# A six-layer local-attention stack on one core: the mask is written into the score banks by ScalarE instead of by two matmuls, and three engines' lists are reordered

## What is computed

```
q, k, v = split(shift_tokens(x) @ Wqkv)        # 16 heads of 64
q, k = l2norm(q) * qs, l2norm(k) * ksc         # then rotary tables, cos and sin part
sim = q @ k2.T * 8                             # windows of 32 queries see 64 keys: the one before and their own
sim = where(mask, -huge, sim)
x = softmax(sim) @ v2 @ Wo + x
x = (a * gelu(gate)) @ W2 + b2 + x             # (a, gate) = layernorm(shift_tokens(x)) @ W1 + b1
```

## Time and profile before

| | us |
|---|---|
| median of 3 runs | 3620.34 (3605.24 to 3626.68) |
| the profiled execution, device time | 3621.26 |
| its span in the profile | 3619.1 |

### The profile page before, as it was taken

One profiled execution on the slowest core, in us unless ns is written; L12 is line 12 of the kernel. 1 busy time (PEld: TensorE's weight loads), 2 busy tenths in 40 slices (PEclk: granted clock), 3 DMA queues, 4 the chain that ended last, 5 costly groups with the idle time before them and its releaser, 6 DMA issues. The chain is left out here.

```text
span 3619.1 us, 152088 instructions
## 1 busy us (share of the span) xinstructions
PE 3322.5 (92%) x64040; PEld 2535.6 (70%) x64040; DVE 2800.4 (77%) x4983; ACT 2482.6 (69%) x3080; POOL 2720.1 (75%) x2152
## 2 busy tenths in 40 slices
PE   6899999999999999998677899999999999999996
PEld 4777777777777777776335777777777777777774
DVE  5778878788878878876447788778888878878883
ACT  4677777777767777775225677777777777777773
POOL 5888888788878878875007888888888888888881
PEclk8999999999999999999889999999999999999998
DMA  3333333333333333332002333333333333333320
GB/s 96 77 83 82 80 83 82 78 86 79 79 84 78 80 87 77 81 88 64 6 0 67 79 85 82 80 84 78 83 86 78 81 83 80 81 83 77 78 74 25
DMA packets 208997, 272.66 MB, mean 75 GB/s; under 512 B 55748, under 2 KB 103744, under 8 KB 208320
## 3 DMA queue, kind: packets, MB, share of 16 engines
q1 hardware_dynamic: 208320, 262.94, 28.2%
HBM read 60.35 MB, written 1.05 MB: 17 GB/s over the span
## 5 line engine op out<-in xcount | busy, mean ns | idle before, releaser
L1240 POOL TENSOR_TENSOR V<-RAWQK,TAB 128x512 f32<-128x512 f32 x768 | 953.2, 1275 | 443.5 <-PE PS L340 434.3
L388 PE MATMUL PS<-WH,XH 128*128 128x512 f32 x1152 | 518.4, 450 | 99.9 <-ACT VS L770 86.3
L770 ACT ACTIVATE VS<-PS 128x1024 f32<-128x1024 f32 x192 | 196.5, 1023 | 481.0 <-PE PS L390 357.2
L1282 POOL TENSOR_TENSOR V<-V,U 128x1024 f32<-128x1024 f32 x192 | 455.6, 2373 | 14.9
L390 PE MATMUL PS<-WL,XH 128*128 128x512 f32 x1152 | 465.5, 404 | 0.0
L389 PE MATMUL PS<-WH,XL 128*128 128x512 f32 x1152 | 464.5, 403 | 0.0
L1266 POOL TENSOR_TENSOR V<-V,U 128x1024 f32<-128x1024 f32 x192 | 457.5, 2383 | 0.0
L1275 POOL TENSOR_TENSOR V<-V,RN 128x1024 f32<-128x1024 f32 x192 | 372.2, 1938 | 93.7 <-DVE RN L918 92.1
L340 PEld LDWEIGHTS PS<-EYE,V 128*128 128x128 f32 x3072 | 348.2, 141 | 110.2 <-issue 99.0
L510 PEld LDWEIGHTS PS<-OT,WO 128*128 128x128 f32 x3072 | 373.6, 192 | 21.4 <-issue 5.1
L340 PE MATMUL PS<-EYE,V 128*128 128x128 f32 x3072 | 371.3, 274 | 10.3 <-ACT OT L777 5.1
(11 more groups left out here) (162 smaller groups left out, 7100.0 us busy)
## 6 DMA issues: line engine op xcount, KB each, us to landing
V<-VS SPq DMA_DIRECT2D x3072, 64.0 KB
ROTB<-c_rot SPq DMA_DIRECT2D x192, 128.0 KB, 2.5
WSTAGE<-wqkv SPq DMA_DIRECT2D x33, 512.0 KB
WO<-wo SPq DMA_DIRECT2D x12, 512.0 KB, 3.8
W<-w SPq DMA_DIRECT2D x12, 341.0 KB, 3.1
QKS<-qks SPq DMA_DIRECT2D x12, 128.0 KB, 3.7
W<-w SPq DMA_DIRECT2D x12, 114.0 KB
RAWQK<-x SPq DMA_DIRECT2D x4, 256.0 KB, 3.7
```

The costliest lines, as they stand in the source:

```text
L388: pe.matmul(o, XH[:, p, :], WH[:, w, cols], start=True, stop=False)
L1240: ins = pool.tensor_tensor(paired(V[:, k])[:, :, :, h * half:(h + 1) * half], split(RAWQK[:, k])[:, :, :, (1 - h) * half:(2 - h) * half], ...
L1282: pool.tensor_tensor(V[:, 1], V[:, 1], U[:, 1], ALU.add).then_inc(k_turned, 1)
```

## The change

- `scores_a` no longer runs the two mask matmuls. ScalarE writes the mask (from the fp32 copy MASKF) into the two score banks in one instruction, `seed_scores`, right behind `keep_queries`, and signals `seeded`; TensorE waits for that. SEED_LAG is 0, so this holds for every chunk.
- `turn` opens each bank once (`start` for the first of four transpositions only).
- The scores stand at the end of TensorE's turn, as those of chunk t-1, and no longer at the head of the next turn.
- VectorE writes the difference (score minus row maximum) into the buffer of probabilities PR in SBUF, after a wait for `p_rows` of the chunk before; the exponential runs in place there. TensorE's queries and the transposition of queries wait for `shifted` where they waited for `exp_done`.
- ScalarE's list: `keep_halo` moves from before the exponential to behind `keep_weights`; `shift` moves from before `ffn_late` to behind it.
- VectorE's list: `cos_keys` is ahead of `add_back`; `cos_queries` is written at the head of the turn, with t-1.
- GpSimd's list: `add_keys` moves ahead of `sin_queries` and `low_part`.

The diff, cut to its core:

```diff
@@ turn (PE)
                 for h in range(NP_):
                     mm = pe.matmul(PS[:, bank + h // 4, (h % 4) * P:(h % 4 + 1) * P], src(h), EYE[:, :],
-                                   is_transpose=True, start=True, stop=True, skip_group_check=True)
+                                   is_transpose=True, start=(h % 4 == 0), stop=True, skip_group_check=True)
@@ queries (PE)
-                    after(use(exp_done, c - 2), use(exp_done, c - 2), use(q_kept, c - 2), use(uq_done, c - 1))
+                    after(use(shifted, c - 2), use(shifted, c - 2), use(q_kept, c - 2), use(uq_done, c - 1))
@@ scores_a (PE)
-                    after(use(q_kept, c), use(uq_done, c + 1), use(exp_done, c - 1), use(exp_done, c - 1))
-                    for r in range(2):
-                        pe.matmul(PS[:, B_S + r, :], EYEB[:, :], rep(MASK[:, 1 if c % CH == 0 else 0, :], [P, NP_, 2 * WIN], 1),
-                                  start=True, stop=False, skip_group_check=True)
+                    after(use(q_kept, c), use(uq_done, c + 1), use(shifted, c - 1), use(shifted, c - 1))
+                    if live(c + SEED_LAG):
+                        pe.wait_ge(seeded, seed_count(inv, c))
...
                     pe.wait_ge(q_kept, count(inv, c))
@@ TensorE's turn
                 for t in range(108):
-                    scores_a(t - 2)
-                    scores_b(t - 2)
                     values(t - 1)
...
                     ffn_third(t - 2)
+                    scores_a(t - 1)
+                    scores_b(t - 1)
@@ new (ACT)
+                def seed_scores(c):
+                    if not live(c) or not live(c + SEED_LAG):
+                        return
+                    act.wait_ge(q_kept, count(inv, c))
+                    act.activation(rows(B_S).rearrange("p r (j k) -> p r j k", k=2 * WIN),
+                                   MASKF[:, 1 if c % CH == 0 else 0, :].unsqueeze(1).unsqueeze(1).broadcast_to([P, 2, NP_, 2 * WIN]),
+                                   ACT.Copy).then_inc(seeded, 1)
@@ exponentials (ACT)
                     act.wait_ge(shifted, count(inv, c))
-                    held(p_rows, count(inv, c - 1))
-                    held(sum_done, count(inv, c - 1))
-                    if inv == 0 and c == 0:
-                        act.wait_ge(w_split, 3)
-                    act.activation(PR[:, :, :].rearrange("p (j r) k -> p r j k", r=2),
-                                   rows(B_S).rearrange("p r (j k) -> p r j k", k=2 * WIN), ACT.Exp).then_inc(exp_done, 1)
+                    act.activation(PR[:, :, :], PR[:, :, :], ACT.Exp).then_inc(exp_done, 1)
@@ ScalarE's turn
                 for t in range(109):
+                    keep_weights(t - 3)
+                    keep_halo(t - 3)
                     copy_queries(t - 1)
...
                     keep_queries(t - 2)
+                    seed_scores(t - 2)
                     square_queries(t - 1)
+                    ffn_late(t - 3)
                     shift(t)
-                    ffn_late(t - 3)
                     keep_values(t - 1)
-                    keep_halo(t - 2)
                     exponentials(t - 2)
                     copy_keys(t)
-                    keep_weights(t - 2)
@@ row_max (DVE)
-                    dve.tensor_tensor(s, s, rep(MX[:, :, :], [P, 2, NP_, 2 * WIN], 3), ALU.subtract).then_inc(shifted, 1)
+                    held(p_rows, count(inv, c - 1))
+                    if inv == 0 and c == 0:
+                        dve.wait_ge(w_split, 3)
+                    dve.tensor_tensor(PR[:, :, :].rearrange("p (j r) k -> p r j k", r=2), s,
+                                      rep(MX[:, :, :], [P, 2, NP_, 2 * WIN], 3), ALU.subtract).then_inc(shifted, 1)
@@ VectorE's turn
                 for t in range(111):
+                    cos_queries(t - 1)
                     row_sum(t - 3)
...
                     norm(t - 1)
+                    cos_keys(t)
                     add_back(t - 4)
-                    cos_keys(t)
                     scale_keys(t - 1)
-                    cos_queries(t)
@@ GpSimd's turn
                 for t in range(109):
+                    add_keys(t - 2)
                     sin_queries(t - 2)
                     low_part(t - 1)
-                    add_keys(t - 2)
                     add_queries(t - 2)
```

More of the change, by code:

```diff
@@ L204, in build @@
         q_rows = sem("q_rows"); k_rows = sem("k_rows"); q_kept = sem("q_kept"); k_kept = sem("k_kept"); halo_kept = sem("halo_kept")
-        scored = [sem("scored%d" % r) for r in range(2)]; shifted = sem("shifted"); exp_done = sem("exp_done"); sum_done = sem("sum_done")
+        scored = [sem("scored%d" % r) for r in range(2)]; seeded = sem("seeded"); shifted = sem("shifted"); exp_done = sem("exp_done"); sum_done = sem("sum_done")
         p_rows = sem("p_rows"); p_kept = sem("p_kept"); v2_even = sem("v2_even"); v2_odd = sem("v2_odd")
@@ L240, in v2_count, with seed_count @@
             return ((inv * NCH + c) // 2 + 1) * V2_INC
+        def seed_count(inv, c):
+            return inv * (NCH - SEED_LAG) + c + 1
         def phase(n):
@@ L423, in turn_queries @@
                     pe.wait_ge(q_scaled, count(inv, c))
-                    after(use(uq_done, c + 1), use(exp_done, c - 1), use(exp_done, c - 1), use(q_kept, c - 1))
+                    after(use(uq_done, c + 1), use(shifted, c - 1), use(shifted, c - 1), use(q_kept, c - 1))
                     turn(lambda h: V[:, 0, 2 * h:2 * h + 2, :].rearrange("p r d -> p (r d)"), B_TQ).then_inc(q_rows, 1)
@@ L447, in scores_a @@
                         return
-                    after(use(q_kept, c), use(uq_done, c + 1), use(exp_done, c - 1), use(exp_done, c - 1))
-                    for r in range(2):
-                        pe.matmul(PS[:, B_S + r, :], EYEB[:, :], rep(MASK[:, 1 if c % CH == 0 else 0, :], [P, NP_, 2 * WIN], 1),
-                                  start=True, stop=False, skip_group_check=True)
+                    after(use(q_kept, c), use(uq_done, c + 1), use(shifted, c - 1), use(shifted, c - 1))
+                    if live(c + SEED_LAG):
+                        pe.wait_ge(seeded, seed_count(inv, c))
+                    else:
+                        for r in range(2):
+                            pe.matmul(PS[:, B_S + r, :], EYEB[:, :],
+                                      rep(MASK[:, 1 if c % CH == 0 else 0, :], [P, NP_, 2 * WIN], 1),
+                                      start=True, stop=False, skip_group_check=True)
                     pe.wait_ge(q_kept, count(inv, c))
```

## The result

The changed kernel is slower: 3709.03 us median, 3620.07 for the kernel before beside it, ratio 1.0241, 95% interval 1.0212 to 1.0271. One of the four executions was disturbed and counts in that median; the ratio goes by the other three (3693.18 to 3717.96 us). The profiled execution is the quickest of them, 3693.18 us with a span of 3690.7, so of the 87 us that the ratio means the two spans show 71.6. Forecast were 3627 us and a range of 3590 to 3660: the time lies outside it.

A forecast was written before the change was run, and what follows sets the result against it. TensorE is busy 92%, but GpSimd's later XL was to cancel its saved 0.52 us per chunk. Unstalled periods +7.0, stalled -2.9, ends +2: in all +6 on 3621.26, so 3627 us; range 3590 to 3660.

The forecast's parts named there:

- XL decides K: GpSimd's low_part, now behind add_keys, delivers XL at P + 8.42 us; TensorE's start of the next keys waits for it.
- K - P: From P, GpSimd starting its sine parts, to K, TensorE starting the next chunk's keys; forecast 8.4 us in turns 0, 2, 3.
- turn 1: Second of a period's four turns: K gains 0.52 us, the exponential ends as before; -0.35 us, bounds -0.52 and -0.2.
- Turn 2, not stalled: Gelu turn in 26 of 48 periods: ScalarE's list is full, the seed delays keep_values; +0.25 us, bounds +0.1 and +0.6.
- the pauses vanish into the new wait: Turn 0: TensorE's pauses inside the scores are absorbed by the wait for XL; lower bound, +0.23 us.
- stalls as many as before: Sign listed for the forecast: the number of stalls stays unchanged.
- +0.05 a period: Turn 3: K - P goes from 8.37 to 8.42 us; bounds 0 and +0.15.
- +0.32 for turn 0: Turn 0: GpSimd's late XL raises short K - P to 8.42 us; mean +0.32 us, bounds +0.23 and +0.5.
- 0.25 us in turn 0: Turn 0: scores wait for ScalarE's seed and start at 813.6 against 813.37, 0.25 us later; the 0.52 us saving is lost.
- the stalled turns: Turns 1 and 2 in 22 of 48 periods, ScalarE waiting for DMAs of values: keep_halo off the exponential's way, -0.5 us together.
- The seed is dear: Rival: ScalarE's seed takes 1.5 us, comes after GpSimd's XL, turn 0 scores 0.7 us later: 3657 us; chance 0.17.
- The clock falls: Rival: TensorE's pauses before K in turn 0 halve its clock, six matmuls dearer by 0.29 us: about 3710; chance 0.04.

The follow-up runs named there:

- the split: Values projection put between the two halves of the scores on TensorE, in the kernel before with keep_halo moved behind keep_weights: 3707.52 us, ratio 1.0207; with the seed besides 3716.21.

## Why the prediction was wrong

**What held.** XL decides K in turns 0 and 3: the medians of K - P are 8.48 and 8.50, forecast 8.42. The seed takes 1.03 (forecast 1.05). In turn 1 the median goes from 9.24 to 8.81, -0.43 for -0.35. Turn 2, not stalled, goes by its lower quartile from 8.38 to 8.69, +0.31 for +0.25. The difference in PR cost nothing. The Trainium skill's rule for ScalarE that was weighed ("VectorE: DVE Perf Modes", TRN2 errata) holds in size: the exponential's median went from 1.024 to 1.058 us as its source moved to SBUF, 0.034 more for the 0.04 worked out from that page.

**The step that failed: the tails.** I read the pauses inside the scores in before, put them down as a property of turn 0, and let the new floor of K - P absorb them ("the pauses vanish into the new wait"). The forecast says "stalls as many as before". They grew from 52.6 to 102.0 us by the plain count and to some 86 without what isn't supply. That it is the missing masks that do it, two pairs of runs show: without masks and seed the pauses grow too (94.4), and with the masks put back beside the seed they fall (102.0 to 61.1). In turn 3 the pauses between P and K went from 5.8 to 29.1 us; that turn was to cost +0.05 a period and cost +0.78. 23.3 of its 34.1 us are pauses, and GpSimd's order alone gives 10.9. The lower clock behind the pauses comes on top there: 30.7 us at that level for 3.4.

**Mis-sized: GpSimd's order.** +0.32 for turn 0 was near (alone it measured +0.39, 17.2 us in 44 turns). That turn 1 and turn 3 would be touched by 0.20 and 0.25, and the rest by 12.8 us instead of 2, was not in the sum.

**Mis-sized: the seed.** I took it as hidden except for 0.25 us in turn 0, which GpSimd would cover. With GpSimd's order in place and TensorE's masks kept, it still cost 33 us: turn 2 +15.5 (ScalarE's list is full; forecast +0.25 a turn for both causes, 0.37 measured for the seed alone), turn 0 +7.3, the rest +8.1. And the price doubles to 61 us when the masks are gone; of this interaction the profiles show a part. Without the masks the seed brings 14 us of pauses (84 of 1.21 us on the mean for 84 of 1.05), with them 7; and without them it brings 8 us at the lower clock, with them none. That is 7 us, and at most 5 by the clock, of 28. **What makes up the remainder isn't settled.** That the scores of turn 0 wait for the seed was forecast, and they do, in all 44 turns; what it costs was not in the sum.

**Right in direction, too small: the halo.** -0.5 in the stalled turns made -11 us; -21 were measured, half of them outside the steady turns.

**The rivals.** "The seed is dear" (3657) named the right culprit by the wrong mechanism: it was to decide from 1.2 us, and at 1.03 us it cost 33 to 70. "The clock falls" (3710) has nearly the time by luck. Its mechanism, a fall in every turn 0 after a wait for XL, didn't come: 5 of the 44 steady turns 0 have a stretch at the lower level, 20.5 us in all. But the clock did fall, in some turns 0 and 3, behind supply pauses, and the mean went from 0.969 to 0.963; that is a part of the loss, by the estimate above up to 24 us, and no run parts it from the pauses. Every undisturbed execution of a kernel without TensorE's masks and without the split has a granted clock of 0.966 or less, every one with them 0.965 or more. No rival said that work taken from the busiest engine might be worth nothing; the run without masks showed just that.

## What to carry to other kernels

Ahead of crediting an engine with work that you take away, look at its waits with no releaser and at where in the program they fall: here 100 us of matmuls were worth 21 at most, in part because TensorE was waiting for its own instructions next. Such a wait isn't of one kind: the profile put the wait for the seed under "issue" as well, and only the end of the seed beside the start of the scores tells them apart. Small instructions are what starves it, and a slow one between them helps only if no one waits for their result. An edit that moves a step on two engines at once should be priced by its parts, since one part can be there just to cover the other's cost. And the only part that paid here was a copy moved by two lines, which the others hid: each part deserves a run of its own.

## What the runs showed of the hardware

I hadn't expected that TensorE's program is brought in during the run, in packets of 16.4 KB, and that this can be the bound: 256 instructions in 1.5 us outrun it, a pause is mostly under 2.5 us and at most 3.1, but up to 4.0 (once, in the kernel with 48 idle instructions per layer; 3.8 in the changed one) if a load of 0.6 MB (WO and QKS) has been issued ahead of it. Behind ten pauses of over 2.3 us in turns 0 and 3 the granted clock fell to the lower level, for 3.4 or 6.8 us. The Trainium skill, "Trainium Architecture — The Big Picture", section "The software stack", has the instruction streams moved into the engines' memory when the program is loaded; taken by itself, that sentence doesn't fit the 507 packets spread over this run. Shifting the program by 64 idle instructions is enough to move the pauses to other turns, so an edit anywhere ahead of a quick stretch can change its time.
